# A new order of the prologue's steps on ScalarE, VectorE and GpSimd in a two-part transformer block

## Chip, core and metric
One NeuronCore of a Trainium2 chip runs the whole kernel. The metric is the device time of one execution in microseconds (us). Engines: TensorE (PE, matrix products and transposes), VectorE (DVE), ScalarE (ACT), GpSimd (POOL), and SyncE (SP), which only issues DMAs.

## What is computed
The input has 4 batches of 1024 tokens of width 512, all float32. A small vector `c` gives six modulation vectors per batch; two of them are gates, bounded away from zero. The reference, cut to what matters:

```python
mod = (silu(c) @ wmod).reshape(4, 6, 1, 512)
sa, ca, ga, sb, cb, gb = (mod[:, i] for i in range(6))
ga = (2*(ga >= 0) - 1) * maximum(abs(ga), 0.25)      # gb the same
h = layernorm(x) * (1 + ca) + sa
q, k = h @ Wq.T, h @ Wk.T                            # rank 64, one score matrix for all heads
attn = softmax(q @ k.T)
x = x + ga * (attn @ (h @ Wv.T)) @ Wo.T
h = layernorm(x) * (1 + cb) + sb
x = x + gb * (h @ sum_of_8_factors / sqrt(8) + bias)
```

As all heads have the same scores, the kernel multiplies Wv and Wo together once (`wvo`), and adds the eight factor matrices up once.

## The kernel before
Products in float32 are made of three products of parts: each operand is split into a rounded `hi` and a rest `lo`, and TensorE adds hi*lo, lo*hi and hi*hi (lines 524 to 526). ScalarE or VectorE rounds the `hi`, VectorE subtracts to get the `lo` (line 1189), so each operand costs two engines a pass.

The tokens are 32 tiles of 128 rows. Batch 0's eight tiles (0 to 7) and tile 8 go through a prologue; then `step(t)` runs for t from 0 on, each attending with tile t's probabilities while it projects tile t+8, and the last steps are written out by hand. Every engine has its own in-order list of instructions, written out by hand for the prologue; the engines meet at semaphores. A step moved within one engine's list changes no other list.

A tile q of x passes through these, here called by the names that the lists use:
- VectorE `moments_of(q)`: `x_sums` and `x_moments` (lines 1192, 1196), after tile pair q//2 was loaded by SyncE (line 321).
- GpSimd `of_x(q)`: `inverse_std`, three small operations (lines 1667, 1669, 1671), the inverse deviation and `nmr`, the shift; for q from 4 to 11 it first waits until tile q-4 was normalized.
- ScalarE `x_row(q)` (line 1052; for tiles 9, 10 and 11 `normalize_x`, line 846): the normalized rows. They need `nmr` of tile q, and for `x_row` the transposes of tile q-2.
- TensorE `transpose_early(q)` (line 530; the three late tiles 9, 10, 11 are transposed inside steps 0, 1 and 2).
- ScalarE `h_of(q)` (line 837): modulation out of PSUM, waits for `h_lo` of tile q-1. VectorE `h_first(q)` (line 1206) rounds it, `h_second(q)` gives `h_lo`.
- TensorE `values_of(q)` (needs `h_lo` of q and the `lo` of the values of tile q-2) and per pair `qk_of(pair)`; ScalarE and VectorE `values_of(q)` and `qk(pair)` take them out of PSUM. `pair_q(0)` lays out the queries of pair 0. `scores` of tile 0, `row_max(0)` and `exponentials(0)` lead into step 0.

TensorE's own list is not touched. Its part around the change is: values 3, transposes 5, values 4, transposes 6, `qk_of(2)`, the other modulation vectors (`other_vectors`, line 551, which `copy_rows` on ScalarE takes out), values 5, transposes 7, values 6, transposes 8, `other_columns`, `qk_of(3)`, values 7, scores of tile 0, step 0 (tile 9's transposes in it), step 1 (tile 10's in it), step 2 (tile 11's).

The factors: SyncE loads factor 0 into `f_sum` and factor 4 into `g_sum`. GpSimd adds the others by accumulating DMAs of its own queue (`add_half`, line 1743; `add_factor(i)` issues two halves of 0.5 MB). Factors 1, 2, 3 go onto `f_sum` and 5, 6, 7 onto `g_sum`; each half must wait until the half before it in its sum has landed:

```python
wait(pool, added[half], 16 * n)      # n additions of this half have landed
```

That wait stands in GpSimd's list, so whatever follows it there waits too. `sum_factors(k)` (line 1750) adds quarter k of both sums; ScalarE's `factor_parts` rounds them in step 2, and GpSimd takes the rest `f_lo` (line 1792), which the first feed-forward product in step 3 needs. `of_x1(t)` is the inverse deviation of the second layer norm. In the DMA views q1 is the queue of SyncE, q0 that of GpSimd.

Of the kernel before, what the change touches and what calls it, by code (L numbers as in the profile page):

```python
# [58 lines left out]
def adaln_block(nc, x, wqk_t, wv, wo_t, factors, bias, c_t, wmod, out):  # L59
# [38 lines left out]
    with ExitStack() as ctx:  # L98
# [731 lines left out]
        def _(act):  # L830
# [10 lines left out]
            def normalize_x(q, u):  # L841
                act.wait_ge(nmr1_done, q + 1)
                wait(act, xt_ps, q)
                if q == TB + 3:
                    act.wait_ge(mod_acc, 2)
                nc.scalar.activation((xb if q == TB + 3 else xn)[:], x_ring[:, q & (2 * TB - 1), :], ACT.Identity,
                                     scale=rstd1[:, q % MOMENTS:q % MOMENTS + 1], bias=nmr1[:, q % MOMENTS:q % MOMENTS + 1]).then_inc(xn_done, 1)
# [37 lines left out]
            def qk(pair):  # L885
                act.wait_ge(qk_acc, pair + 1)
                rounded(qk_hi[:, pair & (PB - 1), :], ps_qk[:, 0:2 * P]).then_inc(qk_hi_done, 1)
                rounded(k_both[0:R, pair & (2 * PB - 1), :], ps_qk[R:2 * R, 0:2 * P]).then_inc(k_hi_done, 1)

            def pair_q(pair):  # L890

                act.wait_ge(qk_hi_done, pair + 1)
                wait(act, s_acc, 2 * pair)
                source = full(qk_hi[0:R, pair & (PB - 1), :])
                rounded(qs_hi[0:R, :], source)
                rounded(qs_hi[R:2 * R, :], source).then_inc(qs_hi_done, 1)

            def exponentials(t):
                act.wait_ge(max_done, t + 1)
                if t and turned_by_pe(t - 1):  # L900
                    act.wait_ge(pt_ps, 2 * pe_turns_of(t))
                elif t:
                    act.wait_ge(p_out, 16 * trips_of(t))
                to, source = probs[:], ps_s[:]
                if not turned_by_pe(t):
                    to = probs[:].rearrange("p (a k r) -> p a k r", a=Q, r=BLK)
                    source = ps_s[:].rearrange("p (k a r) -> p a k r", a=Q, r=BLK)
                nc.scalar.activation(to, source, ACT.Exp, bias=negmax[:, t & 3:(t & 3) + 1],  # L908
                                     accum_out=rowsum[:, t & 3:(t & 3) + 1]).then_inc(exp_done, 1)
# [126 lines left out]
            def wv_upper(k):  # L1036
                act.wait_ge(wv_loaded[k], 16)
                rounded(wv_parts[0][:, k, :], wv_raw[:, k, :]).then_inc(wv_hi_done, 1)

            def wo_upper(k):  # L1040
                act.wait_ge(wo_loaded[k], 16)
                rounded(wo_parts[0][:, k, :], wo_raw[:, k, :]).then_inc(wo_hi_done[k], 1)
# [5 lines left out]
            def x_row(q):  # L1048
                act.wait_ge(nmr1_done, q + 1)
                wait(act, xt_ps, q - 1)  # L1050
                u = q % 2
                nc.scalar.activation(prologue_xn[u], x_ring[:, q, :], ACT.Identity,
                                     scale=rstd1[:, q % MOMENTS:q % MOMENTS + 1], bias=nmr1[:, q % MOMENTS:q % MOMENTS + 1]).then_inc(xn_done, 1)

            def h_of(q):
                modulate_x(q, 0 if q < TB else 1, prologue_x[q % 2])

            def values_of(q):
                values(q, prologue_v[q % 2])
# [6 lines left out]
            wo_upper(1)  # L1066
            act.wait_ge(c_loaded, 16)
            nc.scalar.activation(silu_den[:], c_sb[:], ACT.Exp, scale=-1.0).then_inc(silu_exp, 1)
            wo_upper(2)
            wv_upper(2)  # L1070
            x_row(0)
            wv_upper(3)
            x_row(1)
# [12 lines left out]
            values_of(1)  # L1086
            h_of(3)
            x_row(4)
            h_of(4)
            qk(1)  # L1090
            values_of(2)
            x_row(5)
            x_row(6)
            h_of(5)
            h_of(6)
            values_of(3)
            values_of(4)
            x_row(7)
            copy_rows()
            qk(2)  # L1100
            x_row(8)
            h_of(7)
            values_of(5)
            values_of(6)
            h_of(8)
            pair_q(0)
            qk(3)
            values_of(7)
            exponentials(0)
            normalize_x(TB + 1, 1)  # L1110
            step(0)
            step(1)
            act.wait_ge(mod_t_done, 4)
# [72 lines left out]
        def _(dve):  # L1186
# [47 lines left out]
            def qk(pair):  # L1234
                qk_rest(pair)
                k_rest(pair)

            def pair_q(pair):

                dve.wait_ge(qk_lo_done, pair + 1)  # L1240
                wait(dve, s_acc, 2 * pair)
                source = full(qk_lo[0:R, pair & (PB - 1), :])
                nc.vector.tensor_copy(qs_lo[0:R, :], source)
                nc.vector.tensor_copy(qs_lo[R:2 * R, :], source).then_inc(qs_lo_done, 1)

            def row_max(t):
                dve.wait_ge(s_acc, t + 1)
                nc.vector.tensor_reduce(negmax[:, t & 3:(t & 3) + 1], ps_s[:], AX_X, ALU.max,  # L1248
                                        negate=True).then_inc(max_done, 1)
# [185 lines left out]
            def h_first(q):  # L1435
                h_upper(q, q // 2, q % 2)

            def h_second(q):
                h_rest(q, q % 2)

            def moments_of(q):
                dve.wait_ge(x_loaded[q // 2] if q else x_first, 16)
                wait(dve, nmr1_done, q - MOMENTS + 1)
                x_stats(q, q % 2)

            def values_of(q):
                values(q, prologue_v[q % 2])
# [30 lines left out]
            def other_columns():  # L1478
                dve.wait_ge(mod_tps, 2)
                turned = mod_t_banks[1][:].rearrange("p (c j r) -> p j c r", c=C, r=STRIP)  # L1480
                for i in range(2):
                    nc.vector.tensor_scalar(mod_t[:, :, 2 + i, :].rearrange("p b c -> p c b"),
                                            turned[:, 2 + i, :, 0:B], float(i), None,
                                            ALU.add).then_inc(mod_t_done, 1)
# [35 lines left out]
            h_first(2)  # L1520
            h_second(2)
            qk(0)
            h_first(3)
            h_second(3)
            values_of(1)
            moments_of(6)
            h_first(4)
            qk(1)
            h_second(4)
            values_of(2)  # L1530
            h_first(5)
            h_second(5)
            moments_of(7)
            moments_of(8)
            moments_of(9)
            values_of(3)
            h_first(6)
            h_second(6)
            values_of(4)
            bound_gates()  # L1540
            h_first(7)
            h_second(7)
            qk(2)
            pair_q(0)
            values_of(5)
            values_of(6)
            h_first(8)
            h_second(8)
            qk(3)
            row_max(0)  # L1550
            values_of(7)
            other_columns()
            step(0)
            dve.wait_ge(bias_loaded, 16)
            step(1)
# [106 lines left out]
        def _(pool):  # L1662
# [11 lines left out]
            def of_x(q, u):  # L1674
                if MOMENTS <= q < TB + MOMENTS:
                    wait_alone(pool, pool_passed, xn_done, q - MOMENTS + 1)
                inverse_std(q + 1, q % MOMENTS, mv1, ve1, rstd1, nmr1, mv1_done, ve1_done, rstd1_done, nmr1_done)
# [74 lines left out]
            def last_wv_rest():  # L1752
                pool.wait_ge(wv_hi_done, C)
                nc.gpsimd.tensor_tensor(wv_parts[1][:, C - 1, :], wv_raw[:, C - 1, :], full(wv_parts[0][:, C - 1, :]),
                                        ALU.subtract).then_inc(last_wv_done, 1)

            def wqk_rest():
                pool.wait_ge(wqk_hi_done, 1)
                nc.gpsimd.tensor_tensor(wqk_lo[:], wqk_raw[:], full(wqk_hi[:]), ALU.subtract).then_inc(wqk_lo_done, 1)
# [3 lines left out]
                add_half(i, 1)  # L1763

            last_wv_rest()
            of_x(2, 0)
            wqk_rest()
            of_x(3, 1)
            of_x(4, 0)
            of_x(5, 1)  # L1770
            of_x(6, 0)
            add_factor(1)
            add_factor(5)
            of_x(7, 1)
            of_x(TB, 0)
            of_x(TB + 1, 1)
            add_factor(2)
            add_factor(3)
            add_factor(6)
            add_factor(7)  # L1780
            of_x(TB + 2, 0)
            of_x1(0, 0)
            sum_factors(0)
            sum_factors(1)
            sum_factors(2)
            of_x(TB + 3, 1)
            of_x1(1, 1)
            sum_factors(3)
            pool.wait_ge(bias_loaded, 16)
            for k in range(C):  # L1790
                pool.wait_ge(f_hi_done, k + 1)
# [79 lines left out]
```

## Time and profile before
| | us |
|---|---|
| median of 3 runs | 455.6 |
| lowest and highest of them | 452.86, 457.02 |
| the profiled execution | 454.29 |
| span of its profile | 452.5 |
| TensorE busy in it | 441.0 |
| VectorE, ScalarE, GpSimd busy | 356.4, 319.6, 233.1 |

The rows further down come from that one execution; times in them are microseconds from the start of its span, durations in the grouped views nanoseconds. TensorE's matmul rows overlap (each lasts until its result is out), so the distance between starts tells its pace. What stands in brackets is the engine's idle time before the row and what ended it.

### The profile page before, as it was taken

What the parts mean: (1) busy time and instruction counts of PE and PEld (TensorE: products, weight loads), DVE (VectorE), ACT (ScalarE), POOL (GpSimd) and SP (SyncE); (2) the same over time, 40 slices, a digit from 0 to 9 for tenths busy, and PEclk for the clock granted to TensorE, in tenths of its full rate; (3) what the DMA queues carried; (4) which work ended last, traced back from release to release, by engine and by line L of the source; (5) the groups of instructions that cost most, each with busy time, mean ns of one, the idle gap of its engine ahead of it and who ended that gap; (6) DMA issues with size and microseconds to landing.
All of it is one profiled execution on the core that took longest, in us unless ns stands there. A gap on an engine that the chain in (4) does not pass through costs nothing. (4 is left out here: it accounts for less than half of the span.)

```text
span 452.5 us, 7294 instructions
## 1 busy us (share of the span) xinstructions
PE 441.0 (97%) x2118; PEld 363.6 (80%) x2118; DVE 356.4 (79%) x610; ACT 319.6 (71%) x642; POOL 233.1 (52%) x308
## 2 busy tenths in 40 slices
PE   8999996999999999999999999999999999999996
PEld 7686885888888888888888888887788888887885
DVE  5677654587887978988877978896887877999977
ACT  3676663677978676888868787876878564667761
POOL 1528337262555635466555645465555427168882
PEclk9999998999999999999999999999999999999999
DMA  8999997123477356778596366767687136758423
GB/s 324 391 407 312 218 191 112 48 81 106 141 240 225 116 188 191 250 193 251 168 255 206 116 190 218 233 189 203 181 245 219 48 121 201 215 163 280 128 83 139
DMA packets 77750, 88.05 MB, mean 195 GB/s; under 512 B 5000, under 2 KB 55944, under 8 KB 77200
## 3 DMA queue, kind: packets, MB, share of 16 engines
q1 hardware_dynamic: 73872, 80.51, 57.0%
q0 software_dynamic: 3264, 6.29, 8.0%
q10 hardware_dynamic: 576, 0.79, 0.5%
q8 instruction: 17, 0.28, 0.3%
q14 instruction: 21, 0.17, 0.1%
HBM read 53.49 MB, written 34.10 MB: 194 GB/s over the span
## 5 line engine op out<-in xcount | busy, mean ns | idle before, releaser
L1667 POOL TENSOR_SCALAR ve<-mv 128x1 f32<-128x1 f32 x64 | 21.1, 330 | 164.1 <-DVE mv L1304 115.2
L525 PE MATMUL ps_o<-v_hi,pt_lo 128*128 128x512 f32 x192 | 74.7, 389 | 0.0
L524 PE MATMUL ps_o<-v_lo,pt_hi 128*128 128x512 f32 x192 | 74.7, 389 | 0.0
L526 PE MATMUL ps_o<-v_hi,pt_hi 128*128 128x512 f32 x192 | 74.7, 389 | 0.0
L860 ACT ACTIVATE h_f<-x1b,mod_t 128x128 f32<-128x128 f32 x120 | 53.1, 598 | 5.5 <-DVE x1b L1322 5.3
L1189 DVE TENSOR_TENSOR h_lo<-h_f,h_hi 128x512 fp32r<-128x512 f32 x57 | 42.8, 750 | 8.9 <-ACT h_hi L832 8.6
L524 PE MATMUL ps_v<-wvo_lo,h_hi 128*128 128x512 f32 x112 | 45.5, 406 | 1.1 <-DVE h_lo L1189 1.1
L908 ACT ACTIVATE probs<-ps_s,negmax 128x1024 f32<-128x1024 f32 x32 | 35.4, 1108 | 12.7 <-DVE negmax L1248 12.1
L525 PE MATMUL ps_v<-wvo_hi,h_lo 128*128 128x512 f32 x112 | 44.3, 396 | 0.0
L526 PE MATMUL ps_v<-wvo_hi,h_hi 128*128 128x512 f32 x112 | 44.2, 394 | 0.0
L1669 POOL TENSOR_TENSOR rstd<-ve,minus_half 128x1 f32<-128x1 f32 x64 | 41.3, 646 | 5.3
L860 ACT ACTIVATE h_f<-xb,mod_t 128x128 f32<-128x128 f32 x80 | 35.4, 593 | 10.1 <-DVE xb L1318 9.8
L1248 DVE TENSOR_REDUCE negmax<-ps_s 128x1 f32<-128x1024 f32 x32 | 38.9, 1215 | 4.5 <-PE ps_s L604 4.1
L524 PEld LDWEIGHTS ps_o<-v_lo,pt_hi 128*128 128x128 f32 x192 | 36.0, 188 | 7.6
L526 PEld LDWEIGHTS ps_o<-v_hi,pt_hi 128*128 128x128 f32 x192 | 36.0, 188 | 7.5
L525 PEld LDWEIGHTS ps_o<-v_hi,pt_lo 128*128 128x128 f32 x192 | 36.0, 188 | 7.4
L1189 DVE TENSOR_TENSOR pt_lo<-pb,pt_hi 128x512 fp32r<-128x512 f32 x40 | 33.3, 854 | 3.5 <-ACT pt_hi L832 3.0
L1690 POOL TENSOR_TENSOR ffn<-ffn,gates 128x512 f32<-128x512 f32 x24 | 33.7, 1403 | 3.7 <-issue 3.7
L524 PE MATMUL ps_y<-f_lo,h_hi 128*128 128x512 f32 x88 | 34.4, 391 | 0.5 <-ACT ffn L988 0.5
L832 ACT ACTIVATE v_hi<-ps_v 128x512 fp32r<-128x512 f32 x28 | 16.8, 599 | 25.6 <-PE ps_v L526 25.6
L526 PE MATMUL ps_y<-f_hi,h_hi 128*128 128x512 f32 x88 | 34.3, 389 | 0.0
L525 PE MATMUL ps_y<-f_hi,h_lo 128*128 128x512 f32 x88 | 34.2, 389 | 0.0
(232 smaller groups left out, 1179.2 us busy)
## 6 DMA issues: line engine op xcount, KB each, us to landing
x_blocks<-xn SPq DMA_DIRECT2D x50, 256.0 KB, 2.7
p_blocks<-probs SPq DMA_DIRECT2D x24, 512.0 KB, 3.5
pb<-p_blocks SPq DMA_DIRECT2D x96, 128.0 KB, 3.1
x1b<-x_blocks SPq DMA_DIRECT2D x30, 256.0 KB, 2.9
result<-x_ring SPq DMA_DIRECT2D x15, 512.0 KB, 3.0
xb<-x_blocks SPq DMA_DIRECT2D x20, 256.0 KB, 2.9
x_ring<-in_x SPq DMA_DIRECT2D x18, 256.0 KB, 3.2
wmod<-in_wmod SPq DMA_DIRECT2D x4, 1024.0 KB, 15.4
```

Of the source, the lines that this page charges most:

```text
L524: nc.tensor.matmul(acc, a_hi, b_lo, start=first, stop=False)
L525: nc.tensor.matmul(acc, a_lo, b_hi, start=False, stop=False)
L526: return nc.tensor.matmul(acc, a_hi, b_hi, start=False, stop=last)
L832: return nc.scalar.activation(to, source, ACT.Identity)
L860: last = nc.scalar.activation(to[:, k, :].rearrange("p (c b) -> p b c", b=Q), turned[:, k], ACT.Identity, scale=mod_t[:, b, v + 1, k:k + 1 ...
L908: nc.scalar.activation(to, source, ACT.Exp, bias=negmax[:, t & 3:(t & 3) + 1], accum_out=rowsum[:, t & 3:(t & 3) + 1]).then_inc(exp_done, 1)
L1189: return nc.vector.tensor_tensor(to, whole, full(hi), ALU.subtract)
L1248: nc.vector.tensor_reduce(negmax[:, t & 3:(t & 3) + 1], ps_s[:], AX_X, ALU.max, negate=True).then_inc(max_done, 1)
L1667: nc.gpsimd.tensor_scalar(ve[:, one], mv[:, u, 1:2], EPS, None, ALU.add).then_inc(ve_done, 1)
L1669: nc.gpsimd.tensor_tensor(rstd[:, one], ve[:, one], minus_half[:], ALU.pow).then_inc(rstd_done, 1)
L1690: nc.gpsimd.tensor_tensor(ffn_of(t), ffn_of(t), gates[:, 1, b & 1, :], ALU.mult).then_inc(gated_done, 1)
```

## The change
Only the order of calls within three lists changes, and no call is added or removed. On ScalarE: the weights' `wv` part 2 goes ahead of `wo` part 2; `values_of(2)` ahead of `h_of(4)`; `qk(1)` behind `x_row(6)`; `x_row(7)` ahead of `values_of(3)`; `h_of(6)` behind `values_of(4)`; `qk(2)` ahead of `copy_rows`, and `pair_q(0)` right behind it; `values_of(5)` ahead of `h_of(7)`; `h_of(8)` ahead of `values_of(6)`; tile 9's normalization ahead of `exponentials(0)`. On VectorE and GpSimd as the diff shows.

```diff
@@ scalar @@
-            wo_upper(2)
             wv_upper(2)
+            wo_upper(2)
...
             x_row(4)
+            values_of(2)
             h_of(4)
-            qk(1)
-            values_of(2)
             x_row(5)
             x_row(6)
+            qk(1)
             h_of(5)
-            h_of(6)
+            x_row(7)
             values_of(3)
             values_of(4)
-            x_row(7)
+            h_of(6)
+            qk(2)
             copy_rows()
-            qk(2)
+            pair_q(0)
             x_row(8)
+            values_of(5)
             h_of(7)
-            values_of(5)
+            h_of(8)
             values_of(6)
-            h_of(8)
-            pair_q(0)
             qk(3)
             values_of(7)
+            normalize_x(TB + 1, 1)
             exponentials(0)
-            normalize_x(TB + 1, 1)
@@ vector @@
             qk(0)
+            pair_q(0)
             h_first(3)
             h_second(3)
+            moments_of(6)
             values_of(1)
-            moments_of(6)
+            moments_of(7)
+            values_of(2)
             h_first(4)
+            h_second(4)
             qk(1)
-            h_second(4)
-            values_of(2)
             h_first(5)
             h_second(5)
-            moments_of(7)
+            values_of(3)
             moments_of(8)
             moments_of(9)
-            values_of(3)
+            values_of(4)
             h_first(6)
             h_second(6)
-            values_of(4)
             bound_gates()
             h_first(7)
             h_second(7)
             qk(2)
-            pair_q(0)
             values_of(5)
+            h_first(8)
             values_of(6)
-            h_first(8)
             h_second(8)
             qk(3)
             row_max(0)
+            other_columns()
             values_of(7)
-            other_columns()
@@ gpsimd @@
             last_wv_rest()
+            wqk_rest()
             of_x(2, 0)
-            wqk_rest()
             of_x(3, 1)
+            add_factor(1)
             of_x(4, 0)
             of_x(5, 1)
             of_x(6, 0)
-            add_factor(1)
+            of_x(7, 1)
+            add_factor(2)
             add_factor(5)
-            of_x(7, 1)
             of_x(TB, 0)
             of_x(TB + 1, 1)
-            add_factor(2)
+            add_factor(6)
+            of_x(TB + 2, 0)
+            add_factor(7)
             add_factor(3)
-            add_factor(6)
-            add_factor(7)
-            of_x(TB + 2, 0)
             of_x1(0, 0)
+            of_x(TB + 3, 1)
             sum_factors(0)
             sum_factors(1)
             sum_factors(2)
-            of_x(TB + 3, 1)
+            sum_factors(3)
             of_x1(1, 1)
-            sum_factors(3)
```

`TB` is 8, so `of_x(TB)` is tile 8 and `of_x(TB + 2)` is tile 10.

## Rows read from the trace of the kernel before
**Rows 1.** The page, part 1: busy us, share of the span, instructions.
```profile
PE 441.0 (97%) x2118; PEld 363.6 (80%) x2118; DVE 356.4 (79%) x610; ACT 319.6 (71%) x642; POOL 233.1 (52%) x308
```
**Rows 2.** TensorE's waits, whole span: us in total, times, longest us.
```profile
PE ps_o L530 <- issue: 3.8, 1, 3.8
PE ps_v L524 <- DVE h_lo L1189: 1.1, 2, 0.7
```
**Rows 3.** Timeline of TensorE, 33 to 75 us: start, us, operation.
```profile
33.87 0.40 PE L524 MATMUL ps_t<-wvo_lo,h_hi 128*128 128x512 f32 x1
...
51.57 0.60 PE L530 MATMUL ps_t<-ident,xn 128*128 128x128 f32 x4
...
52.36 0.36 PE L524 MATMUL ps_qk<-h_lo,wqk_hi 128*128 128x256 f32 x1
...
70.34 0.28 PE L526 MATMUL ps_qk<-h_hi,wqk_hi 128*128 128x256 f32 x1
74.47 0.74 PE L530 MATMUL ps_o<-ident,xn 128*128 128x128 f32 x4 [3.84 <-issue]
```
**Rows 4.** Timeline of ScalarE, 46 to 99 us.
```profile
46.84 0.81 ACT L1052 ACTIVATE xn<-x_ring,nmr,rstd 128x512 f32<-128x512 f32 x1
...
67.86 0.19 ACT L908 ACTIVATION_READ_ACCUMULATOR probs<-ps_s,negmax 128x1 f32 x1
73.56 0.81 ACT L846 ACTIVATE xn<-x_ring,nmr,rstd 128x512 f32<-128x512 f32 x1 [5.51 <-POOL nmr L1671]
...
98.14 0.81 ACT L868 ACTIVATE xn<-x_ring,nmr,rstd 128x512 f32<-128x512 f32 x1 [1.09 <-POOL nmr L1671]
```
**Rows 5.** Timeline of GpSimd, 36 to 97 us.
```profile
36.09 2.64 POOL L1743 DMA_DIRECT2D f_sum<-in_factors  x2 [0.24 <-issue]
...
41.29 0.23 POOL L1667 TENSOR_SCALAR ve<-mv 128x1 f32<-128x1 f32 x1
...
42.38 0.26 POOL L1671 TENSOR_SCALAR nmr<-mv,rstd 128x1 f32<-128x1 f32 x1 [0.21 <-POOL rstd L1669]
...
47.82 1.20 POOL L1743 DMA_DIRECT2D f_sum<-in_factors  x1 [0.39 <-DMA f_sum<-in_factors]
...
70.89 1.20 POOL L1743 DMA_DIRECT2D wmod<-in_factors  x1 [1.34 <-DMA wmod<-in_factors]
...
73.26 0.26 POOL L1671 TENSOR_SCALAR nmr<-mv,rstd 128x1 f32<-128x1 f32 x1 [0.21 <-POOL rstd L1669]
...
91.30 5.05 POOL L1792 TENSOR_TENSOR f_lo<-f_sum,f_hi 128x512 fp32r<-128x512 f32 x4
```
**Rows 6.** Stretches: length, busy PE, PEld, DVE, ACT, POOL, granted clock, DMA share, GB/s.
```profile
70.70:74.40 3.70, 0.00 (x0) 0.00 (x0) 0.70 (x2) 0.84 (x2) 2.96 (x6) 1.00 1.04 157
74.40:78.00 3.60, 3.53 (x12) 2.89 (x13) 1.42 (x3) 3.44 (x9) 3.39 (x5) 0.56 0.63 116
```
**Rows 7.** Timeline of VectorE, 31 to 52 us.
```profile
31.99 0.68 DVE L1189 TENSOR_TENSOR v_lo<-ps_t,v_hi 128x512 fp32r<-128x512 f32 x1
32.59 0.69 DVE L1192 BATCH_NORM_STATS2 stats<-x_ring 128x6 f32<-128x512 f32 x1
33.81 0.18 DVE L1196 BATCH_NORM_AGGREGATE mv<-stats 128x2 f32<-128x6 f32 x1 [0.54 <-DVE stats L1192]
...
51.02 0.69 DVE L1189 TENSOR_TENSOR h_lo<-h_f,h_hi 128x512 fp32r<-128x512 f32 x1
```
**Rows 8.** Timeline of SyncE's queue: the issue of x tiles 6 and 7.
```profile
14.70 0.43 SPq L321 DMA_DIRECT2D x_ring<-in_x  x1
```
**Rows 9.** DMA issues in 14.6 to 15.1 us: KB each, us to landing.
```profile
x_ring<-in_x SPq DMA_DIRECT2D x1, 512.0 KB, 16.5
```
**Rows 10.** DMA issues in 36.0 to 36.9 us: KB each, us to landing.
```profile
f_sum<-in_factors POOLq DMA_DIRECT2D x1, 512.0 KB, 8.9
```
**Rows 11.** DMA queues in 38 to 40 us, all of them: packets, MB, share.
```profile
q1 hardware_dynamic: 398, 0.78, 105.3%
```
**Rows 12.** DMA queues in 41 to 44 us, GpSimd's: packets, MB, share.
```profile
q0 software_dynamic: 301, 0.59, 107.9%
```

More of the change, by code:

```diff
@@ L1068, in _ @@
             nc.scalar.activation(silu_den[:], c_sb[:], ACT.Exp, scale=-1.0).then_inc(silu_exp, 1)
+            wv_upper(2)
             wo_upper(2)
-            wv_upper(2)
             x_row(0)
```

## The prediction
> **What bounds the kernel now.** I read the page's busy line first: TensorE is busy for 97% of the span [rows 1], so a change to the other engines' order can only give back time in which TensorE idles. TensorE's list of waits comes second: over the whole span one wait of 3.8 us stands out, and the entry after it adds up to 1.1 us in two waits [rows 2]. The timelines of TensorE, ScalarE and GpSimd then follow it back, in that order. TensorE ends the queries and keys of pair 4 at 70.6 and starts the transposes of tile 10 at 74.47 [rows 3]. ScalarE sits idle for 5.51 us before it normalizes tile 10 at 73.56, because GpSimd's `nmr` of tile 10 is missing [rows 4]. GpSimd has that at 73.26 + 0.26 = 73.5, because it first had to issue the second half of factor 7, which waited for factor 6's addition until 70.89 [rows 5]. The stretches give the second part of the price: the granted clock is 0.56 over 74.4 to 78.0, right after the idle 3.7 us, a mixture of 1.2 GHz and 2.4 GHz [rows 6].
>
> **What the moved tile 10 gives back.** In the new GpSimd order tile 10 stands behind factor 6 and ahead of factors 7 and 3. Factor 6 needs only factor 5 to have landed, some 10 us after its issue (chain below: about 60 us), so `nmr` of tile 10 is there at about 63 even in my late case. ScalarE normalizes it at 68.05, when the exponentials end [rows 4], 0.8 us; TensorE, free at 70.6, finds it. The other waits of that transpose were met before, as TensorE resumed 0.1 us after ScalarE's row ended. Gain: 74.47 - 70.62 = 3.8 us, and the clock: 3.6 us at 0.56 do 2.0 us of work at full clock, 1.6 us lost [rows 6]. Together 5.4 us. Behind 78 us the list has no wait of TensorE longer than 0.7 us [rows 2], so what is gained here arrives at the end whole.
>
> **What the other moves cost.** All times are those of the trace of before.
>
> Weights' low part of queries and keys ahead of tile 2 on GpSimd: one 128x512 operation, 1.26 us by the four that take 5.05 [rows 5]. Tile 2's `nmr` may come up to 1.26 us later, before ScalarE asks for it; bounds 0 and 1.3, I take 0, since its input is ready 1 us before tile 2's moments are.
>
> VectorE: moments of tile 6 go ahead of `values_of(1)`. TensorE needs that low part at 33.87 [rows 3]. VectorE comes to it at 31.99 [rows 7]; a pair of moments takes 32.59 to 33.99 = 1.4 at worst, the subtraction 0.69, so 34.1: bounds 0 and 0.3, and with the data in time I take 0. The data: x pair 3 was issued at 14.70 [rows 8] and took 16.5 us [rows 9], 31.2, in time by 0.8 us. The remaining swaps on ScalarE and VectorE (weights, `qk`, `pair_q(0)`, `h_of(8)`, normalization of tile 9, `other_columns`) move operations of 0.3 to 1.5 us within stretches where TensorE never waits. They can lose or win 0.3 us between them; I take 0.
>
> The sums of the factors now come after tile 11, four in one go, and tile 1's second deviation after them: `f_lo` starts about 0.8 us later against the rest, 92.1 instead of 91.30 [rows 5]. Behind it stand tile 12's deviation and ScalarE's 98.14 row, which already waited 1.09 us [rows 4]. ScalarE's next product that TensorE reads is `probs` for its attention, over 2 us ahead of need. Bounds 0 and 0.8; I take 0, and this is what is late next.
>
> **The price that I do expect: tile 8.** GpSimd now issues factor 1 at about 26.4, right after tile 3, then tiles 4 to 7 (done at about 36.6), then factor 2 and factor 5, and only then tiles 8 and 9. Factor 2 waits for factor 1 to land, and GpSimd's queue stands still behind that wait. When does it land? Before, the two halves were issued from 36.09 [rows 5]; the first took 8.9 us [rows 10], and the second released factor 2's second half at 47.82 [rows 5]. Over 38 to 40 us only q1 (SyncE's loads) moves, at 105% of the engines; q0 (GpSimd's) has no packet, though its first half was issued 2 us before [rows 11]. At 41 to 44 us q0 moves 0.59 MB in 3 us, at 108% [rows 12]. So the additions wait until the loads have drained, at about 40, whenever they are issued; issued at 26.4 they land hardly sooner. The loads themselves are unchanged in number.
>
> At 0.2 MB per us, a half of 0.5 MB takes 2.6 us: from 40.3 the second half lands at 45.6 plus 0.5 = 46.1 at best, and at 47.8 as before at worst. I take 46.5. Then come three issues (factor 2's second half, factor 5's two): four took 36.09 to 41.29 = 5.2 us [rows 5], so three are 3.9, or 3.6 at the 1.20 of a lone one: start of tile 8 at 50.1, its `nmr` 1.35 us later (41.29 to 42.64), 51.5. Before, tile 8's row was normalized at 46.84 without waiting [rows 4].
>
> How late is it? ScalarE's order is tile 8's row (0.7 us), `values_of(5)` (0.5), `h_of(7)` (1.5), then VectorE's rounding and subtraction (0.46 and 0.69, the latter at 51.02 [rows 7]), then TensorE's `qk_of(3)`, which ran at 52.36 [rows 3]: 4.0 us with the hand-overs. So `nmr` is wanted by 48.3, and 51.5 is 3.2 us late. TensorE pays 3.2 us between 51.57 and 52.36, in two waits (before tile 8's transposes and before `qk_of(3)`). Bounds: landing at 46.1 with quick issues gives 2.4 us, at 47.8 with slow ones 4.8; no price at all if factor 1 has landed by 43. Tile 10 behind all this: factor 5 is issued at about 49, lands by 59, factor 6 out at 61, tile 10 ready by 63.
>
> Sum: -5.4 + 3.2 = -2.2 us. The profiled execution took 454.29 us with a span of 452.5, so 452.1 and 450.3. The median shown is 455.6, 1.3 above that execution; the forecast goes by the median: 453.4.
>
> The Trainium skill says, in DMA: Bandwidth & Descriptors, section Queues, rings and completion order, that each DMA engine takes turns among the rows that have work, a packet at a time. By it GpSimd's additions would not have to wait for SyncE's loads to drain. The trace of 38 to 40 us speaks against it here, with 398 packets of q1 and none of q0, but the stretch is short. It is the second rival.
>
> **The rivals.**
> A, as above, the likeliest: 453.4. For it: the row without a packet of q0.
> B, equal shares: factor 1's data start 2 us after its issue, at 28.6, and take turns with the loads. x pair 3 then lands up to 2.6 us later (28.6 to 31.2 doubled), 33.8, and VectorE's moments of tile 6 stand in front of `values_of(1)`: moments to 34.9, low part to 35.6, TensorE's 33.87 becomes 35.7: 1.8 us. Factor 1 lands by about 39, tile 8 in time. -5.4 + 1.8 = -3.6: 452.0. Against it: rows 11.
> C, neither: the additions start early enough, or in the gaps, without holding x pair 3. -5.4: 450.2. It needs factor 1's landing by 43, 3 us ahead of what I work out.
> D, slower: tile 8 late and the clock falling with it. The place is TensorE's `qk_of(3)`; the one wait of 3.7 us in the trace was followed by 1.6 us lost to the clock. Here 4.8 + 1.6 = 6.4 against 5.4 gained: +1.0, 456.6. The point from which it decides is `nmr` of tile 8 later than 52.1 (48.3 + 3.8) if the clock falls, 53.7 if it does not. Against it: the idle time is cut in two by the transposes of tile 8.
> That the change misses its aim, tile 10 still late, would need tile 10's `nmr` after 68: 5 us of margin, so 2 in 100, counted under D.
>
> **How the numbers follow.** A 0.55, B 0.15, C 0.18, D 0.12. A measurement of this kernel tells about 1% (4.6 us) from no change: below 451.0 is faster, above 460.2 slower. C lies below that in 0.8 of its cases (0.14), A and B reach it in about 0.1 of theirs and by the spread of three runs of before (452.86 to 457.02), together 0.10: 0.24. Slower by over 1% needs D and something more: 0.04. The rest, 0.72, is within 1%. The range goes from C less half a us, 449.7, to D, 456.8, and leaves out less than 2 in 10. A's own range is 451.8 to 454.8.
>
> **What would show it.** Right: no wait on tile 10's transposes, a granted clock of 1.0 over 70 to 80 us, TensorE waits of some 3 us at about 52, GpSimd waiting for `f_sum` from 37 until 45 to 47 us, q0 silent until about 40. Wrong: q0 packets at 29 to 38 us (B or C); tile 8's `nmr` before 48.3 and no wait at 52 (C); a new wait at 34 us on `v_lo` of tile 1 (B); a clock below 1.0 at 55 us (D); any new wait after 80 us, where I count on cover.

## The result, and the profile after

The changed kernel takes 451.15 us (median of 7 runs, 449.52 to 453.42) against 454.79 us (7 runs, 452.86 to 457.02). The ratio is 0.9917 with a 95% interval of 0.9887 to 0.9946, so 3.8 us less (2.5 to 5.1). The forecast was 453.4 and 2.2 us less; it started from the median of 455.6 that it had. The sign and the main gain were right; the price set against it was too high, for a reason that turned out to be false, and two smaller facts were missed. The measured time lies below the 451.8 to 454.8 that the forecast gave for its own likeliest case.

TensorE's waits in the changed kernel, whole span (us in total, times, longest us), to be held against [rows 2]:

```profile
PE ps_t L530 <- issue: 1.4, 1, 1.4
PE ps_v L524 <- DVE h_lo L1189: 1.2, 2, 0.7
...
PE ps_qk L524 <- DVE qk_lo L1189: 0.8, 1, 0.8
```

The wait of 3.8 us is gone. Two are new: 0.8 us at `qk_of(3)` and 1.4 us at a transpose. The timeline of TensorE shows where (start, us, operation):

```profile
53.18 0.35 PE L524 MATMUL ps_qk<-h_lo,wqk_hi 128*128 128x256 f32 x1 [0.76 <-DVE qk_lo L1189]
...
71.14 0.28 PE L526 MATMUL ps_qk<-h_hi,wqk_hi 128*128 128x256 f32 x1
71.41 0.63 PE L530 MATMUL ps_o<-ident,xn 128*128 128x128 f32 x4
...
93.19 1.06 PE L530 MATMUL ps_t<-ident,probs 128*128 128x128 f32 x8 [1.45 <-issue]
```

Read it by anchors (the starts of the same operation in two kernels), since a wait shows only where the delay comes out. Before, the transposes of tile 8 started at 51.57 and `qk_of(3)` at 52.36, pair 4 ended at 70.6 and tile 10's transposes started at 74.47 [rows 3]. Now `qk_of(3)` is 0.8 us later than before, and tile 10's transposes, 0.15 us after pair 4, are 3.1 us earlier. The granted clock stays up behind them (length, busy PE, PEld, DVE, ACT, POOL, granted clock, DMA share, GB/s), where [rows 6] had 1.00 and 0.56:

```profile
70.70:74.40 3.70, 3.70 (x23) 3.08 (x21) 2.19 (x6) 3.61 (x9) 3.70 (x4) 1.00 0.54 76
74.40:78.00 3.60, 3.60 (x17) 3.00 (x16) 2.70 (x4) 2.61 (x6) 2.09 (x4) 1.00 1.13 196
```

So by the scores of tile 2 the changed kernel is 4.7 us ahead: 5.5 gained at tile 10, 0.8 lost at tile 8. First the kernel before, then the changed one:

```profile
79.28 0.39 PE L603 MATMUL ps_s<-k_both,qs_lo 128*128 128x512 f32 x1
```

```profile
74.62 0.39 PE L603 MATMUL ps_s<-k_both,qs_lo 128*128 128x512 f32 x1
```

The wait in step 3 gives back 1.2 (the same transposes start at 96.63 before, with 0.23 of wait, and at 93.19 now), 3.4 us remain. The two profiled executions differ by only 2.5 us at the end, the medians by 3.6. Most of what the profiles lose after step 3 lies behind 300 us: from 300 to 430 us TensorE idles 1.1 us before and 1.8 now, and from 100 to 300 us not at all. The other kernels below idle 0.2 to 1.3 us there, though no edit touches that part, and two profiles of one kernel differ by 0.3. The cause of this stays open.

GpSimd's timeline tells why tile 10 was only just in time, against [rows 5]:

```profile
26.47 2.63 POOL L1743 DMA_DIRECT2D f_sum<-in_factors  x2 [0.28 <-issue]
...
37.37 1.26 POOL L1743 DMA_DIRECT2D f_sum<-in_factors  x1 [1.10 <-DMA f_sum<-in_factors]
...
41.43 1.19 POOL L1743 DMA_DIRECT2D f_sum<-in_factors  x1 [2.80 <-DMA f_sum<-in_factors]
44.47 2.42 POOL L1743 DMA_DIRECT2D wmod<-in_factors  x2 [1.84 <-DMA wmod<-in_factors]
...
48.52 0.26 POOL L1671 TENSOR_SCALAR nmr<-mv,rstd 128x1 f32<-128x1 f32 x1 [0.22 <-POOL rstd L1669]
...
68.75 0.45 POOL L1667 TENSOR_SCALAR ve<-mv 128x1 f32<-128x1 f32 x1 [8.82 <-DVE mv L1196]
...
70.49 2.49 POOL L1743 DMA_DIRECT2D wmod<-in_factors  x2
72.00 3.43 POOL L1743 DMA_DIRECT2D f_sum<-in_factors  x2
```

Three things are to be seen. The first half of factor 1 has landed by 37.4 and the second by 41.4, not at 46.5. Tile 8's `nmr` ends at 48.8, held up last by factor 4's load (the 1.84 us before 44.47). And GpSimd idles 8.8 us for tile 10's moments: VectorE makes them in step 0, at 68.35, so with these lists nothing could have had that `nmr` at 63. The trace of the kernel before already had them there:

```profile
67.55 0.18 DVE L1196 BATCH_NORM_AGGREGATE mv<-stats 128x2 f32<-128x6 f32 x1
```

Factors 7 and 3, queued behind tile 10 on GpSimd, go out together at 70 to 75 us.

### The profile page after: what moved, and what is told of

Its sections match the earlier page's. It is cut to its first block and busy times, and to the rows that moved or that the text cites. A ratio compares the mean times of both kernels' runs of the same rounds, so it can differ in the third digit from the quotient of the medians.

```text
span 450.0 us, 7294 instructions
## 1 busy us (share of the span) xinstructions
PE 439.2 (98%) x2118; PEld 361.6 (80%) x2118; DVE 356.1 (79%) x610; ACT 319.5 (71%) x642; POOL 234.8 (52%) x308
## 5 line engine op out<-in xcount | busy, mean ns | idle before, releaser
L1669 POOL TENSOR_TENSOR rstd<-ve,minus_half 128x1 f32<-128x1 f32 x64 | 42.2, 660 | 5.3
L1189 DVE TENSOR_TENSOR pt_lo<-pb,pt_hi 128x512 fp32r<-128x512 f32 x40 | 32.2, 830 | 3.2 <-ACT pt_hi L832 2.8
L526 PE MATMUL ps_y<-f_hi,h_hi 128*128 128x512 f32 x88 | 34.3, 389 | 0.0
L1701 POOL TENSOR_TENSOR x_ring<-ffn,x_ring 128x512 f32<-128x512 f32 x24 | 31.5, 1312 | 3.6 <-POOL ffn L1690 3.4
```

Source lines behind the costliest of these rows:

```text
L526: return nc.tensor.matmul(acc, a_hi, b_hi, start=False, stop=last)
L1189: return nc.vector.tensor_tensor(to, whole, full(hi), ALU.subtract)
L1669: nc.gpsimd.tensor_tensor(rstd[:, one], ve[:, one], minus_half[:], ALU.pow).then_inc(rstd_done, 1)
L1701: nc.gpsimd.tensor_tensor(tile, ffn_of(t), tile, ALU.add).then_inc(y_done, 1)
```

## The experiments

Eleven runs of ten kernels were made. Each kernel is a reordering of lines of one of the two, except `kept_busy`, which adds work. Idle time of TensorE is 80 us less its busy time over 20 to 100 us of the profiled execution.

**Tile 8's deviation between factors 2 and 5, on the changed kernel.**

```diff
             add_factor(2)
+            of_x(TB, 0)
             add_factor(5)
-            of_x(TB, 0)
             of_x(TB + 1, 1)
```

> The changed kernel with tile 8's deviation between factors 2 and 5. Theory 1 (TensorE's 0.76 us wait before qk_of(3) comes from tile 8's nmr, which stands behind the wait for factor 4's load): nmr of tile 8 by 45 us instead of 48.8, the wait at 53 us gone, 0.8 us less than the changed kernel, ratio to before 0.990. Rival (the wait comes from ScalarE's and VectorE's new order, h_of(7) behind values_of(5)): the wait stays at 0.5 us or more and the ratio at 0.992.

Measured: ratio 0.9875 (0.9852 to 0.9898). Tile 8's `nmr` is there at 44.4 us:

```profile
44.11 0.26 POOL L1671 TENSOR_SCALAR nmr<-mv,rstd 128x1 f32<-128x1 f32 x1 [0.56 <-POOL rstd L1669]
```

The wait before `qk_of(3)` is gone from the list. So that wait was tile 8's, and not the new order of ScalarE and VectorE. The profile also showed what I had not expected: the wait in step 3 fell from 1.45 to 0.3 us, though its own lines had not been touched.

**Factor 3 ahead of tile 10, on the changed kernel.**

```diff
             add_factor(6)
+            add_factor(3)
             of_x(TB + 2, 0)
             add_factor(7)
-            add_factor(3)
```

> The changed kernel with factor 3 ahead of tile 10's deviation, factor 7 still behind it. Theory 1 (factors 3 and 7, issued together at 70 to 75 us, fill the DMA engines to 83 us, so that the store of the first second-norm tile takes 7.3 us instead of 2.3 and everything behind it is late in step 3): the store takes under 4 us, TensorE's wait of 1.45 us at 93 us falls to 0.3 or less, 1.2 us less than the changed kernel, ratio 0.989. Rival (the wait comes from GpSimd's order: the four sums in one go block VectorE's add, 1.47 us instead of 0.69, and delay what follows): the store gets faster but the wait at 93 us stays above 1 us.

Measured: ratio 0.9876 (0.9854 to 0.9898). The issues of DMAs (KB each, us to landing), first the changed kernel's store of the first tile of the second norm, then the same one here:

```profile
x_blocks<-xn SPq DMA_DIRECT2D x1, 256.0 KB, 7.3
```

```profile
x_blocks<-xn SPq DMA_DIRECT2D x1, 256.0 KB, 2.8
```

The wait in step 3 came down to 0.2 us:

```profile
91.89 1.06 PE L530 MATMUL ps_t<-ident,probs 128*128 128x128 f32 x8 [0.23 <-issue]
```

GpSimd's four sums still stand in one block in this kernel, so the order of the sums is not the cause. The addition that the rival names became quicker too (0.83 us instead of 1.47), which leaves the rival a foothold; the rows of the changed kernel take it away. Behind that addition VectorE idles 1.32 us before it comes to the load, so the addition's length was inside cover. The chain in the changed kernel, on VectorE and ScalarE, is this:

```profile
86.56 0.69 DVE L1189 TENSOR_TENSOR pt_lo<-ps_t,pt_hi 128x512 fp32r<-128x512 f32 x1 [1.32 <-ACT pt_hi L832]
...
88.37 0.71 DVE L1322 STREAM_TRANSPOSE x1b<-x1b 128x512 f32<-128x512 f32 x1 [1.12 <-DMA x1b<-x_blocks]
```

```profile
89.12 1.77 ACT L860 ACTIVATE h_f<-x1b,mod_t 128x128 f32<-128x128 f32 x4 [1.15 <-DVE x1b L1322]
...
91.91 1.09 ACT L908 ACTIVATE probs<-ps_s,negmax 128x1024 f32<-128x1024 f32 x1
```

The store shares the DMA engines with factors 7 and 3, the load behind it starts 5 us late, VectorE and ScalarE each wait 1.1 us for it, and tile 3's exponentials, queued behind that, hold up TensorE's transposes at 93.19. The surprise of the first experiment is in the same chain. With tile 8 moved, everything up to the store ran 1 us earlier; the store took 6.8 us and the load behind it 2.6, instead of 7.3 and 3.1, so the load landed 2 us earlier and VectorE had nothing to wait for:

```profile
86.31 0.71 DVE L1322 STREAM_TRANSPOSE x1b<-x1b 128x512 f32<-128x512 f32 x1
```

An equal shift of 1 us would have left the wait as it was; the 1 us by which the two transfers became shorter took it away. Why they became shorter is not shown.

**Both moves, twice.**

> Both moves. If the two waits are separate and both on TensorE's path, their gains add up: 2.0 us less than the changed kernel, ratio 0.987, no wait of TensorE over 0.7 us between 20 and 430 us. If one hides the other, no better than the better one of them.

> The same kernel as both_ahead once more, to see what a repeat is worth. By TensorE's idle time (2.0 us less than the changed kernel over 20 to 100 us) the ratio should be 0.987; the first time gave 0.9892. If the repeat stays above 0.989, time is given back behind 100 us, and the idle time of TensorE over 300 to 430 us shows it.

Measured: 0.9892 (0.987 to 0.9914) and, the same kernel again, 0.9876 (0.9848 to 0.9904). TensorE's idle time over 20 to 100 us was the same both times, 0.95 and 0.97 us, against 2.9 in the changed kernel, 1.0 with tile 8 moved and 1.55 with factor 3 moved. So the two gains do not add up. Tile 8's move takes away both waits and leaves factor 3's move almost nothing; factor 3's move takes away its own, and 0.6 us stay at `qk_of(3)`. The expected 2.0 us were reached in idle time, but the measured times do not tell the three kernels apart: 449.1 us with tile 8 moved, 449.0 with factor 3 moved, 449.6 and 449.2 with both. Over 300 to 430 us the two profiles of the kernel with both moves idle 0.5 and 0.75 us. The first ratio, higher than expected, was not repeated by the second.

**Only the late part of GpSimd's list, on the kernel before.**

```diff
             add_factor(2)
-            add_factor(3)
             add_factor(6)
-            add_factor(7)
             of_x(TB + 2, 0)
+            add_factor(7)
+            add_factor(3)
             of_x1(0, 0)
+            of_x(TB + 3, 1)
             sum_factors(0)
             sum_factors(1)
             sum_factors(2)
-            of_x(TB + 3, 1)
-            of_x1(1, 1)
             sum_factors(3)
+            of_x1(1, 1)
```

> The kernel before with only the late part of GpSimd's new list: factor 2, factor 6, tile 10, factors 7 and 3, tile 11 ahead of the four sums. Theory 1 (all the gain is tile 10 and the clock after it, the front part only costs): tile 10's transposes without a wait over 0.5 us, granted clock 1.0 over 70 to 80 us, no wait at 53 us, a wait near 1.4 us at about 93 us; 454.8 - 5.4 + 1.2 = 450.6, ratio 0.991. Rival (the earlier factor 1 is needed for tile 10 to be in time): factor 6 goes out late and tile 10 waits 1 us or more, ratio 0.994 or above.

Measured: ratio 0.9898 (0.9875 to 0.9922), 450.13 us. These few lines give all that the change gives, within the intervals; the earlier factor 1 is not needed for tile 10. Idle time is 1.7 us, 0.9 of it in step 3.

**The three lists apart.** GpSimd's new list under the old ones of the other two, and the reverse:

> GpSimd's new list with ScalarE's and VectorE's lists of before. Theory 1 (the whole effect is GpSimd's): tile 10 without its long wait, ratio 0.990 to 0.993; tile 8's nmr at about 49 as in the changed kernel, and the wait at qk_of(3) smaller than 0.8 us, since h_of(7) stands ahead of values_of(5) here; factor 2 goes out at 42 us instead of 37, because tile 7's moments come at 40. Rival (the three lists only work together): a new wait of TensorE over 1 us in the prologue, ratio 0.995 or more.

> ScalarE's and VectorE's new lists with GpSimd's of before. Theory 1: they move operations within cover, tile 10 still waits 3.8 us and the granted clock drops after it, ratio 1.000 within 0.003. Rival: they give 0.5 us or more by themselves, ratio 0.998 or less, and TensorE is ahead of before by that at 60 us.

Measured: 0.990 (0.9856 to 0.9944) for GpSimd's alone, with a wait of 1.2 us at `qk_of(3)`, more than I expected rather than less: tile 7's moments hold factor 2 back to 42.9 there, and tile 8's `nmr` comes at 50.0. ScalarE's and VectorE's alone: 1.0036 (1.0013 to 1.0059), slower by 1.6 us (0.6 to 2.7). I had expected no effect. TensorE waits 6.9 us for tile 10 in that kernel, 3.1 more than before:

```profile
PE ps_o L530 <- issue: 6.9, 1, 6.9
```

Its GpSimd list is that of before, but in VectorE's new list tile 8's moments come later. GpSimd waits 3.2 us for them, and factor 2 goes out behind them:

```profile
45.09 0.22 POOL L1667 TENSOR_SCALAR ve<-mv 128x1 f32<-128x1 f32 x1 [3.18 <-DVE mv L1196]
...
49.31 2.49 POOL L1743 DMA_DIRECT2D f_sum<-in_factors  x2 [0.17 <-issue]
```

Before, factor 2's first half went out at 46.18. The last issue that stands ahead of tile 10 is late by the same 3.1 us, at 74.03 instead of 70.89 [rows 5]. A reordering that moves nothing on TensorE's own path had moved the queue that did. That the measured times show only about half of the wait's growth is not explained.

**When does GpSimd's DMA queue move?** The forecast hung on this. Factor 1 issued earlier, ahead of tile 3's deviation, and later, behind tile 5's:

```diff
             of_x(2, 0)
+            add_factor(1)
             of_x(3, 1)
-            add_factor(1)
```

> The changed kernel with factor 1 issued ahead of tile 3's deviation, at about 21 us instead of 26.5. Queue theory 1 (a newly filled q0 waits 4 to 5 us from its issue while q1 is full, then both alternate packet for packet): q0's first packet at 25 to 26 us, the loads of x tiles 6 and 7 land 1 us or more after 31.4, VectorE's moments of tile 6 wait for them, and TensorE waits at 34 to 35 us. Queue theory 2 (q0 moves only after the loads with 8 KB rows have passed): first packet still at 31 to 32 us, no wait at 34.

```diff
             of_x(3, 1)
-            add_factor(1)
             of_x(4, 0)
             of_x(5, 1)
+            add_factor(1)
             of_x(6, 0)
```

> The changed kernel with factor 1 issued behind tile 5's deviation, at about 29.3 us. Queue theory 1: q0's first packet at 33.4 to 34.4 us. Queue theory 2: at 31.6 to 32. The forecast's theory (q0 silent until the loads have drained at 40) is wrong either way if packets come before 38. Factor 1 lands about 2 us later than in the changed kernel, tile 8 is later by as much unless factor 4's load sets it; wait at qk_of(3) between 0.8 and 3 us.

Issued at 20.90, q0's first packets come in the window from 25 to 26 us; then it has as many packets as q1, over 26 to 29 us (packets, MB, share):

```profile
q0 software_dynamic: 25, 0.05, 27.5%
```

```profile
q1 hardware_dynamic: 99, 0.80, 66.2%
q0 software_dynamic: 99, 0.20, 36.3%
```

In the changed kernel, issued at 26.47, the first packets come at 31.2 to 31.3, and over 32 to 36 us:

```profile
q0 software_dynamic: 260, 0.50, 68.0%
q1 hardware_dynamic: 258, 0.53, 39.7%
```

Issued at 29.60, nothing until 34.3, then over 35 to 36 us:

```profile
q0 software_dynamic: 63, 0.13, 69.3%
q1 hardware_dynamic: 63, 0.13, 38.6%
```

Queue theory 1 holds in all three: q0 starts 4.5 to 4.8 us after the issue while q1 is full, and from then on both move packet for packet, whatever q1's packets hold. The changed kernel has a fourth case: factor 2's first half, issued at 37.37 beside a full q1, moves from 41.8 on, 4.4 us later; over 41.0 to 41.8 q0 has no packet at all. In the kernel before, issued at 36.09, q0's first packets come at 40.1 to 40.2, and SyncE's loads thin out from 40.2 on. There the drain and the start fall together, and I took one for the cause of the other; in the other cases q1 was full when q0 started. A single execution of f1_later took 452.1 us, with a wait of 1.8 us at `qk_of(3)`, since the halves of factor 1 landed 2.3 and 3 us later.

One of f1_earlier took 455.05 us; it is rival B of the forecast, made real:

```profile
PE ps_t L524 <- DVE v_lo L1189: 4.1, 1, 4.1
```

```profile
36.30 0.69 DVE L1192 BATCH_NORM_STATS2 stats<-x_ring 128x6 f32<-128x512 f32 x1 [4.35 <-DMA x_ring<-in_x]
...
37.25 0.66 DVE L1189 TENSOR_TENSOR v_lo<-ps_t,v_hi 128x512 fp32r<-128x512 f32 x1
```

The load of x tiles 6 and 7 lands at 36.3, VectorE's moments wait 4.35 us for it ahead of `values_of(1)`, and TensorE waits 4.1 us. The granted clock then fell, as it had before behind 3.8 us of waiting [rows 6]:

```profile
38.00:40.00 2.00, 1.95 (x5) 1.58 (x6) 1.82 (x5) 1.08 (x2) 1.54 (x4) 0.57 1.05 409
```

In the changed kernel q0 started at 31.2 to 31.3, just as that load landed (14.62 + 16.7 = 31.3). It escaped the collision by some tenths of a microsecond.

**The price of the clock, on the kernel before.**

```diff
+                pe.wait_ge(rows_copied, 2)
+                for _ in range(15):
+                    nc.tensor.matmul(ps_y[:], wvo_hi[:, 0, 0:P], wvo_hi[:, 0, :], start=True, stop=True)
                 pe.wait_ge(attn_done, 1)
                 transpose_x(TB + 2, late_x_banks[TB + 2])
```

> The kernel before, with 15 products of 128x512 into an unused bank of PSUM, 3.4 us, put into TensorE's wait for tile 10; their result is thrown away. Theory 1 (the forecast's second term: the drop of the granted clock after the 3.8 us wait costs 1.6 us by itself): the granted clock stays 1.0 over 74 to 78 us, scores of tile 2 start 1.4 to 1.6 us earlier against the transposes of tile 10, ratio 0.9965. Rival (the clock's drop is hidden behind ScalarE and VectorE, which are the slower side right there): the clock stays 1.0 and the ratio is 1.000.

Measured: ratio 0.996 (0.9937 to 0.9984), 1.8 us less (0.7 to 2.9) for doing 3.6 us of useless work. The stretches that answer to [rows 6], both at full clock, and TensorE's rows:

```profile
70.70:74.40 3.70, 3.55 (x17) 2.60 (x15) 0.85 (x2) 0.00 (x0) 1.99 (x3) 1.00 0.78 138
74.40:78.00 3.60, 2.39 (x13) 2.08 (x14) 0.34 (x1) 3.21 (x8) 3.22 (x6) 1.00 0.90 152
```

```profile
70.67 3.59 PE L716 MATMUL ps_y<-wvo_hi 128*128 128x512 f32 x15
75.61 0.63 PE L530 MATMUL ps_o<-ident,xn 128*128 128x128 f32 x4 [1.36 <-issue]
...
78.83 0.39 PE L603 MATMUL ps_s<-k_both,qs_lo 128*128 128x512 f32 x1
```

From tile 10's transposes to tile 2's scores it takes 3.2 us here and 4.8 before (74.47 to 79.28): 1.6 us, the forecast's term. The changed kernel, with the clock at 1.00, takes 3.2 as well (71.41 to 74.62). The measured gain agrees with the term, and its interval leaves out the rival's 1.000, but it is too wide to size the term by itself. In this one profile the scores of tile 2 start only 0.45 us earlier than before, since GpSimd's last issue ahead of tile 10 came at 72.03 instead of 70.89, though no instruction ahead of it differs between the kernels. So profiles of two executions seem to differ by up to 1.1 us in that queue, which the shift of 3.1 us in the kernel with the two lists alone exceeds.

**The best order that I can name.** The late part alone, with factor 3 ahead of tile 10:

> The kernel before with only the late part of GpSimd's list changed, and factor 3 ahead of tile 10's deviation: nothing is issued early, so no wait at 53 us, and factor 7 alone behind tile 10, so no wait in step 3. Theory 1: TensorE's idle time over 20 to 100 us falls to about 1 us, as with both moves on the changed kernel, ratio 0.988 within 0.002. Rival (the new front of the three lists is worth something that this lacks): ratio 0.992 or more.

Measured: ratio 0.9871 (0.9848 to 0.9894), 449.14 us, 1.0 us of idle time over 20 to 100 us. It beats the kernel before by 5.9 us (4.8 to 6.9), and the changed one by 2 us as the medians stand; the two ratios' intervals overlap slightly, so the lead over the changed kernel is not certain. It is no better than the other mended orders, which it equals with far fewer moved lines. The lists' new front is not needed.

## Why the forecast was right, and where it was wrong

*What bounds the kernel.* Right. TensorE's one long wait, followed back to factor 6's landing, was the place, and late_only shows that it was nearly the whole of it.

*The gain at tile 10, 5.4 us.* Right in size: 5.5 by the anchors. Both terms stand, the wait and the clock, and kept_busy shows the second by itself, 1.6 us by its anchors. The reason given for its safety was wrong: "`nmr` of tile 10 is there at about 63 even in my late case", with "5 us of margin". VectorE aggregates tile 10's moments only in step 0, at 68.35 (67.55 before). The `nmr` came at 70.5, and TensorE lost 0.15 us. I had followed the wait on GpSimd and not asked when its input is made. A margin should be worked out from the latest input of the moved step, not from the one just removed.

*The price at tile 8, 3.2 us.* The place was right (the wait is there, and tile8_ahead removes it), and the size was wrong: 0.8 to 1.0 us. The step that failed is "the additions wait until the loads have drained, at about 40, whenever they are issued". Its only evidence was a stretch of 2 us without a packet of q0 [rows 11]. The runs show in its place a start 4.0 to 4.8 us after the issue and even turns from there. Landing at 41.4 instead of 46.5 takes 5 us off; only 2.7 of them reached tile 8's `nmr` (48.8 against 51.5), mainly because factor 4's load, now sharing the engines, landed at 44.2 instead of 37.8 and held factor 5 for 1.84 us. The working had a slip besides: its best case, 46.1 + 3.6 + 1.35 - 48.3 (the landing, three issues, the `nmr`, and the time by which it is wanted), is a price of 2.75 us and not 2.4. The Trainium skill says (DMA: Bandwidth & Descriptors, section Queues, rings and completion order) that an engine takes turns among the rows a packet at a time. The traces agree once q0 has started, 99 packets against 99; how long one turn is, these counts do not show. I had weighed the rule too low. That rule says nothing of when a queue starts, which was 4.0 to 4.8 us after the issue.

*The rivals.* The result lies between A and C, nearest B's number (452.0) and by none of their mechanisms alone. B's sharing was real, but it began as the load landed, at 31.3, and not at 28.6. f1_earlier, where it began at 25.4, shows the collision at 4.1 us, more than twice the 1.8 that I gave: q1 fell from about 0.41 to 0.27 MB per us from then on. The clock fell behind that wait, which B's price had left out. D's clock drop at tile 8 did not occur: the wait was 0.8 us and the clock stayed at 1.0. C's condition, factor 1 landed by 43, was met, and tile 8 was still late.

*Step 3, taken as covered.* Wrong, by 1.2 us. I named the deviation of tile 12 as next late. It was the store of the second norm's first tile, beside 2 MB of additions, of which factor 3's had been moved from 55 to 72 us and factor 7's from 68 to 70 us. The forecast counted the issues that tile 10 was moved ahead of, and not where their transfers would then fall.

*The other moves, 0.* Right within the change: TensorE was 0.2 us ahead at 48 us. acts_only says that this holds only together with GpSimd's new list.

The sum in the forecast's own form is thus -5.5 + 0.8 + 1.2 = -3.5 us, against 3.8 less as measured. The forecast came as near as it did partly by luck: the price at tile 8 was 2.4 us too high, and the 1.2 us of step 3, which it put at nothing, made up for half of that. Its time of 453.4 missed by 0.8 us more, since seven runs of the kernel before gave 454.79 where it had 455.6 from three. And the 3.5 is not a close account either, as the two profiled executions differ by 2.5 us at the end.

## What to carry to other kernels

When a step is moved ahead of a wait, look up when its own input is made: it cannot be earlier than that, and whatever is now queued behind it waits for that input too. Where DMAs are pushed back, draw their new place on the time axis and ask which small transfer lies there; here 2 MB of background additions turned a 2.3 us store into 7.3 us. And an empty stretch of a queue says when it did not move, not why: it takes a second issue time to tell a fixed start from a wait for another queue.

## What the runs showed of the hardware

A DMA of GpSimd's queue started 1.9 us after its issue when it had the engines alone (issued at 68.34, first packets at 70.2 in the kernel before; 70.49 and 72.4 in the changed one). It took 4.0 to 4.8 us while SyncE's queue was full, at five different issue times (20.90, 26.47, 29.60, 36.09 and 37.37 us). From there both queues moved equal numbers of packets, so the share in bytes followed the packets' size: 0.20 against 0.80 MB over 3 us with q1's 8 KB rows, 0.50 against 0.53 MB over 4 us with rows of 2 KB.

VectorE's addition of two operands in SBUF (the on-chip memory) slows down beside GpSimd's sums: 0.69 us before with none beside it, 1.47 in the changed kernel, where the sums start at 81.67.

```profile
82.02 1.47 DVE L1295 TENSOR_TENSOR x_ring<-attn,x_ring 128x512 f32<-128x512 f32 x1
```

The same addition took 0.83 us with factor 3 moved and 1.03 us with tile 8 moved, where it met the sums at other points, so its price depends on how the two fall together. It was inside cover here. The Trainium skill (SBUF — State Buffer, section Who interferes with whom) says that a VectorE instruction with two inputs in SBUF and a GpSimd instruction that reads SBUF contend for one shared read interface, and that the order of issue decides which of them waits. The rows agree that the two slow each other; which of them waits by the order of issue no run here isolates.
